# Softmax weights times context in a three-layer kernel: one fp32 product rewritten as three fp32r products on split operands, from chunk 6 on

## The chip, the cores and the metric

One NeuronCore of a Trainium2 chip runs the whole program. The metric is the device time of one execution in microseconds (us); less is better. The engines are TensorE (PE, with its weight loads as PEld), VectorE (DVE), ScalarE (ACT), GpSimd (POOL) and SyncE (SP, which here only issues DMAs). Each engine works through its own list of instructions strictly in order; they are tied together by semaphores.

## The reference

Three layers act on `x` (4 batches of 128 tokens, 512 wide). The second (16-head causal attention on compressed features) and the third (a mixture of 16 experts with shared blocks) follow on the first; the change is in the first, cross attention on a context of 2048 rows of 384 per batch:

```
query = LN(x) @ Wq + bq ; key = ctx @ Wk + bk ; value = ctx @ Wv + bv
weights = softmax(query @ key.T / sqrt(512))
x = x + weights @ value
```

The kernel multiplies the softmax weights with the raw context first (128x2048 by 2048x384 for each batch) and with `Wv` afterwards. It is this product, weights times natural context, that the change rewrites.

## The kernel before

**Numbers.** Inputs are fp32. A matmul on fp32 operands is listed as two records in the trace. Elsewhere the kernel splits both operands into a high part, rounded to fp32r, and a low part, the rest, and sums three fp32r products (`split_mm`, L1580: high x low, high x high, low x high). ACT makes the high parts by a copy, DVE (sometimes POOL) the low parts by subtraction.

**Chunks.** The context is handled in 16 chunks g of 512 rows (4 to a batch). Each chunk is loaded twice by SP: transposed (`ring_T`, 4 places, L481) for the scores, and natural (`ring`, 3 places, L474) for the product. Scores use split operands; the product uses plain fp32: the transposed softmax weights `wT` (two buffers) times `ring`, for k in 0..3 (L1898).

**Steps.** All engines run through the same loop, `for step in range(1, TAIL)`, with TAIL = 21, each with its own list for a step. In step s, PE transposes the weights of chunk s-5 into bank `B_W` (`chunk_T`, L1843), computes the scores of chunk s-1 (`chunk_scores`), and near the end of the step multiplies the product of chunk s-5 (L1898). ACT casts the high parts of chunk s (`chunk_hi`, L752), copies `B_W` to `wT` (L894), and takes the exponents of a chunk (`chunk_weights`, L826). DVE makes the low parts of chunk s (`chunk_lo`, L1283) and adds the row constant and takes the maximum of the scores (L1392).

**Batch and head work inside the steps.** Every fourth step a batch has all its chunks. Its sums are transposed and split (`sums_hi` on ACT, L835; `sums_lo` on DVE, L1333; in steps 9, 13, 17), multiplied by `Wv` (`attended`), added to `x` (`cross_added` on DVE, L1323; steps 10, 14, 18) with the moments of the middle layer norm; POOL takes the inverse root (`inverse_root`, L598), DVE applies it (`normalise`, L1079) and PE transposes the rows (`rows_T`, L1589). One step later come `compress`, `moments_2`, `inverse_root_2` (POOL, L620), `normalise_2` and `compressed_T` (PE, L1779; steps 11, 15, 19), then keys, queries and values. From step 13 on each step also has one unit u of 4 heads: `pair_scores` for two units at a time (L1738), masks and maximum on DVE, `unit_exp` on ACT (L852), `unit_weights` on POOL (L627), `unit_T` on PE (also through `B_W`), `unit_copy` on ACT. In step 17 ACT casts the output weights `wo_w` (L734) and DVE makes their low part (L1055).

**Orders that matter.** ACT's list for a step is: high part of the attended rows, `chunk_hi` 0 and 1 (and 2 before step 13), copy of wT, `sums_hi`, `chunk_hi` 2 (from step 13 on), exponents, `unit_copy`, casts, `unit_exp`, `rows_hi`. DVE's is: `chunk_lo`, `cross_added`, `sums_lo`, masks, `normalise`, the scores' maximum, `chunk_lo` 2, `moments_2`, `rows_lo`, and so on. SP's list alternates the loads of transposed chunk g and natural chunk g-6; each waits for its place to be free, and what is behind it waits too.

The staging buffer `raw` has two halves; weights go through it. Its second half holds nothing from the low part of `W_D` (step 6) to `load_expert(1)` after the loop.

Of the kernel before, what the change touches and what calls it, by code (L numbers as in the profile page):

```python
# [25 lines left out]
P = 128  # L26
F32 = mybir.dt.float32
F32R = mybir.dt.float32r
# [8 lines left out]
def layer_program(nc, x, ctx_in, ctxT_in, wqT, wkT, wv, wd, wu, woT, experts, bq, bk, bv, gate, bias_e,  # L37
# [41 lines left out]
    with ExitStack() as es:  # L79
# [9 lines left out]
        def sem(name):  # L89
            return es.enter_context(nc.semaphore(name))  # L90
# [88 lines left out]
        ring_T = at("ring_T", [P, RING_T, TC, CHUNK], ring_at + RING * KT * TD * 4)  # L179
        sc = at("sc", [P, 2, NKEY], s_at)  # L180
# [178 lines left out]
        ulo_first, dlo_first = sem("ulo_first"), sem("dlo_first")  # L359
        u_lo_pool, d3_in = sem("u_lo_pool"), sem("d3_in")  # L360
# [50 lines left out]
        POOL_LO = (2, 3, 4)  # L411

# [48 lines left out]
        def _(sp):  # L461
# [19 lines left out]
            def load_chunk_T(g):  # L481
                if g >= RING_T:
                    sp.wait_ge(cTlo_ok, low_parts(g - RING_T))
                    if pool_parts(g - RING_T):
                        sp.wait_ge(cTlo_pool, pool_parts(g - RING_T))
                sp.dma_start(ring_T[:, g % RING_T], ctxT_in[g].rearrange("p (t n) -> p t n", t=TC)).then_inc(ctxT_at[g % RING_T], 16)
# [33 lines left out]
            load_expert(0)  # L520
            load_expert(1)
# [49 lines left out]
        def _(pool):  # L571
# [42 lines left out]
            for g in POOL_LO:  # L614
                pool.wait_ge(cThi_ok, TC * (g + 1))
                nc.gpsimd.tensor_tensor(cT[:, g % 2, 1, TC - 1, :], ring_T[:, g % RING_T, TC - 1, :], f32(cT[:, g % 2, 0, TC - 1, :]),
                                        ALU.subtract).then_inc(cTlo_pool, 1)
# [23 lines left out]

            for step in range(1, TAIL):
                if (b := batch_at(step, POST + 1)) is not None:
                    inverse_root(norm_no["middle", b])
                if (b := batch_at(step, POST + 2)) is not None:
                    inverse_root_2(b)
                if (u := unit_at(step, 1)) is not None:
                    unit_weights(u)
                if (b := batch_at(step, WO_STEP)) is not None:
                    last_rows(b)  # L650
# [78 lines left out]
        def _(act_e):  # L729
# [17 lines left out]
            def chunk_hi(g, t):  # L747
                if t == 0:
                    act_e.wait_ge(ctxT_at[g % RING_T], 16 * (g // RING_T + 1))
                if g >= 2 and t == 0:  # L750
                    act_e.wait_ge(s_mm, g - 1)
                copy(cT[:, g % 2, 0, t, :], ring_T[:, g % RING_T, t, :]).then_inc(cThi_ok, 1)  # L752
# [75 lines left out]

            def attended_hi(b):
                act_e.wait_ge(a_mm, b + 1)  # L830
                copy(aT(b, 0), bank[B_A][:]).then_inc(ahi_ok, 1)
# [48 lines left out]
            for step in range(1, TAIL):  # L880
# [9 lines left out]
                if 0 <= g < G:  # L890
                    act_e.wait_ge(wT_mm, g + 1)
                    if g >= 2:
                        act_e.wait_ge(o_mm, g - 1)
                    copy(wT[:, g % 2, :], bank[B_W][:]).then_inc(wT_ok, 1)  # L894
# [148 lines left out]
        def _(dve):  # L1043
# [237 lines left out]
            def chunk_lo(g, t):  # L1281
                dve.wait_ge(cThi_ok, TC * g + t + 1)
                V_.tensor_tensor(cT[:, g % 2, 1, t, :], ring_T[:, g % RING_T, t, :], f32(cT[:, g % 2, 0, t, :]),  # L1283
                                 ALU.subtract).then_inc(cTlo_ok, 1)

# [291 lines left out]
        def _(pe):  # L1577
# [163 lines left out]
            def unit_T(u, step=TAIL):  # L1741
                pe.wait_ge(hw_ok, u + 1)
                if step - LAG < G:
                    pe.wait_ge(wT_ok, step - LAG + 1)
                else:
# [86 lines left out]
            def chunk_T(step):  # L1832
                g = step - LAG
                if 0 <= g < G:
                    b, c = divmod(g, NCH)
                    pe.wait_ge(w_ok, g + 1)
                    if (u := unit_at(step, 3)) is not None:
                        pe.wait_ge(hwT_ok, u + 1)
                    elif g >= 1:
                        pe.wait_ge(wT_ok, g)  # L1840
                    for k in range(KT):
                        o = c * CHUNK + k * P
                        last = nc.tensor.transpose(bank[B_W][:, k * P:(k + 1) * P], sc[:, b % 2, o:o + P], ident[:])  # L1843
# [24 lines left out]
            for step in range(1, TAIL):  # L1868
# [22 lines left out]
                if 0 <= g < G:  # L1891
# [276 lines left out]
```

## Time and profile before

| | us |
|---|---|
| three runs | 354.63, 355.23, 355.56 |
| median | 355.23 |
| profiled execution, its own time | 355.39 |
| its span, first to last instruction | 353.7 |
| granted TensorE clock, mean over the span | 0.990 |

Durations in the rows below come from the one profiled execution, whose time is the 355.39 us. Starts are counted from the start of its span. PE rows overlap, since matmuls are pipelined: the cost of one is the distance to the next start, not its listed duration. The chain that ended last follows the work back from the last instruction, at each step to what released it.

### The profile page before, as it was taken

What the parts mean: (1) busy time and instruction counts of PE and PEld (TensorE: products, weight loads), DVE (VectorE), ACT (ScalarE), POOL (GpSimd) and SP (SyncE); (2) the same over time, 40 slices, a digit from 0 to 9 for tenths busy, and PEclk for the clock granted to TensorE, in tenths of its full rate; (3) what the DMA queues carried; (4) which work ended last, traced back from release to release, by engine and by line L of the source; (5) the groups of instructions that cost most, each with busy time, mean ns of one, the idle gap of its engine ahead of it and who ended that gap; (6) DMA issues with size and microseconds to landing.
All of it is one profiled execution on the core that took longest, in us unless ns stands there. A gap on an engine that the chain in (4) does not pass through costs nothing.

```text
span 353.7 us, 7041 instructions
## 1 busy us (share of the span) xinstructions
PE 336.4 (95%) x2554; PEld 235.2 (67%) x2554; DVE 240.7 (68%) x475; ACT 189.4 (54%) x428; POOL 95.6 (27%) x114
## 2 busy tenths in 40 slices
PE   6999889999999999999899899999999999999996
PEld 4998656677777766767789789787544444444344
DVE  2875869665489728748975469980547777778486
ACT  2356666533577476565777454402246777777520
POOL 3600310000001311226575140004457544432000
PEclk9899999999999999999899999999999999999999
DMA  6984398985333227118023470799835633321663
GB/s 232 400 336 165 139 396 356 418 290 216 120 126 111 92 90 259 69 39 348 0 89 124 149 267 16 294 380 391 341 110 184 196 120 120 121 92 61 238 268 119
DMA packets 17185, 69.70 MB, mean 197 GB/s; under 512 B 2816, under 2 KB 3328, under 8 KB 14592
## 3 DMA queue, kind: packets, MB, share of 16 engines
q1 hardware_dynamic: 12768, 56.93, 43.0%
q0 software_dynamic: 3520, 11.54, 9.4%
q10 hardware_dynamic: 864, 0.79, 0.7%
q8 instruction: 21, 0.34, 0.4%
q14 instruction: 12, 0.10, 0.1%
HBM read 61.91 MB, written 7.34 MB: 196 GB/s over the span
## 4 chain that ended last, share of the span: by engine, by line
PE 76%; DVE 12%; ACT 6%; issue 3%; DMA 2%; POOL 0%; ACTq 0%; DVEq 0%
PE bank L2075 10%; PE bank L2043 10%; PE bank L1582 8%; PE bank L1898 8%; PE bank L1584 8%; PE bank L1583 8%; PE bank L2012 3%; PE bank L1791 2%; PE bank L2054 2%; PE bank L2086 2%; DMA raw<-in_wkT 2%; DVE cT L1283 2%; PE bank L1748 2%; PE bank L1843 2%; PE bank L1589 1%
## 5 line engine op out<-in xcount | busy, mean ns | idle before, releaser
L1898 PE MATMUL bank<-ring,wT 128*128 128x384 f32 x128 | 44.0, 487 | 0.7 <-ACT wT L894 0.7
L2075 PE MATMUL bank<-WX,hsT 128*32 128x512 f32 (+1 forms) x128 | 38.2, 598 | 0.0
L2043 PE MATMUL bank<-WX,xsT 128*32 128x256 f32 (+1 forms) x256 | 37.9, 380 | 0.0
L1283 DVE TENSOR_TENSOR cT<-ring_T,cT 128x512 fp32r<-128x512 f32 x45 | 31.0, 732 | 6.7 <-ACT cT L752 6.7
L1898 PEld LDWEIGHTS bank<-ring,wT 128*128 128x128 f32 x128 | 23.6, 190 | 14.2 <-ACT wT L894 0.9
L2043 PEld LDWEIGHTS bank<-WX,xsT 128*32 128x32 f32 x256 | 17.9, 110 | 21.0 <-issue 10.7
L1514 DVE COPY down_copy<-WX 128x1024 f32 x32 | 21.0, 695 | 15.8 <-PE bank L2075 15.8
L2075 PE MATMUL bank<-down_copy,hsT 128*32 128x512 f32 x192 | 30.7, 598 | 0.0
L752 ACT CAST cT<-ring_T 128x512 fp32r<-128x512 f32 x48 | 27.0, 619 | 6.5 <-PE bank L1584 6.3
L2043 PE MATMUL bank<-up_copy,xsT 128*32 128x256 f32 x384 | 30.4, 379 | 0.0
L688 POOL DMA_INDIRECT xs<-x_rows,from_row x20 | 20.0, 1001 | 37.1 <-DVE to_row L1237 25.2
L598 POOL TENSOR_TENSOR rstd<-var,mhalf 128x1 f32<-128x1 f32 x12 | 7.5, 626 | 72.3 <-DVE var L1069 72.3
L695 POOL DMA_INDIRECT y_rows<-ys,to_row x16 | 17.1, 1068 | 33.7 <-ACT ys L1000 33.7
L1507 DVE COPY up_copy<-WX 128x1024 f32 x32 | 21.1, 696 | 7.4 <-PE bank L2043 3.5
L1024 ACT COPY down_copy<-WX 128x1024 f32 x16 | 16.8, 1049 | 17.1 <-PE bank L2075 17.1
L1492 DVE COPY xsT<-bank 128x512 f32<-128x512 f32 x20 | 13.7, 685 | 14.8 <-PE bank L2012 14.8
L1582 PE MATMUL bank<-cT,qk_h 128*128 128x512 f32 x48 | 20.2, 420 | 2.4 <-DVE cT L1283 1.7
L1016 ACT COPY up_copy<-WX 128x1024 f32 x16 | 16.8, 1048 | 4.7 <-PE bank L2043 3.4
L1584 PE MATMUL bank<-cT,qk_l 128*128 128x512 f32 x48 | 18.8, 392 | 0.0
L1583 PE MATMUL bank<-cT,qk_h 128*128 128x512 f32 x48 | 18.8, 392 | 0.0
L2075 PEld LDWEIGHTS bank<-WX,hsT 128*32 128x32 f32 x128 | 7.4, 109 | 16.5 <-issue 16.5
L1582 PE MATMUL bank<-xT_l,u_w 128*128 128x256 f32 (+2 forms) x56 | 17.9, 320 | 0.0
(296 smaller groups left out, 892.3 us busy)
## 6 DMA issues: line engine op xcount, KB each, us to landing
WX<-in_experts SPq DMA_DIRECT2D x16, 1024.0 KB, 7.0
ring_T<-in_ctxT SPq DMA_DIRECT2D x16, 768.0 KB, 6.8
ring<-in_ctx SPq DMA_DIRECT2D x16, 768.0 KB, 5.0
WX<-y_rows SPq DMA_DIRECT2D x4, 1024.0 KB, 9.4
raw<-in_experts SPq DMA_DIRECT2D x3, 1024.0 KB, 4.8
raw<-in_wqT SPq DMA_DIRECT2D x4, 256.0 KB, 5.6
res<-in_x SPq DMA_DIRECT2D x4, 256.0 KB, 7.8
raw<-in_woT SPq DMA_DIRECT2D x1, 1024.0 KB, 4.9
```

The costliest lines, as they stand in the source:

```text
L688: nc.gpsimd.indirect_dma_start(out=xs[:, s % NXS, :], out_offset=None, in_=x_rows, in_offset=bass.IndirectOffsetOnAxis(ap=from_row[:, s:s ...
L695: nc.gpsimd.indirect_dma_start(out=y_rows, out_offset=bass.IndirectOffsetOnAxis(ap=to_row[:, s:s + 1], axis=0), in_=ys[:, s % NYS, :], in_ ...
L752: copy(cT[:, g % 2, 0, t, :], ring_T[:, g % RING_T, t, :]).then_inc(cThi_ok, 1)
L1283: V_.tensor_tensor(cT[:, g % 2, 1, t, :], ring_T[:, g % RING_T, t, :], f32(cT[:, g % 2, 0, t, :]), ALU.subtract).then_inc(cTlo_ok, 1)
L1507: V_.tensor_copy(up_copy[place(g, q)][:], WX[:, bass.ds(expert * (2 * HALF), HALF)]).then_inc(up_copied, 1)
L1514: V_.tensor_copy(down_copy[place(g, q)][:], WX[:, bass.ds(expert * (2 * HALF) + HALF, HALF)]).then_inc(down_copied, 1)
L1582: mm(dst, a[0], b[1], start=start, stop=False)
L1583: mm(dst, a[0], b[0], start=False, stop=False)
L1584: return mm(dst, a[1], b[0], start=False, stop=stop)
L1898: last = mm(bank[B_O][:, 0:TD], wT[:, g % 2, k * P:(k + 1) * P], ring[:, g % RING, k, :], start=(c == 0 and k == 0), stop=(c == NCH - 1 an ...
L2043: last = mm(bank[B_H[g % 2]][q * SLOT:(q + 1) * SLOT, 0:IC * P], xsT[:, g % 2, c * P + q * SLOT:c * P + (q + 1) * SLOT], w, start=c == 0, ...
L2075: last = mm(bank[B_Y[g % 2]][q * SLOT:(q + 1) * SLOT, :], hsT[:, g % 2, m * P + q * SLOT:m * P + (q + 1) * SLOT], w, start=m == 0, stop=m ...
```

## The change

From chunk 6 on (`SPLIT = 6`) the product of weights and context is made by `split_mm` from four operands: high and low part of wT, high and low part of the natural chunk. Chunks 0 to 5 stay as they are. The high parts of the context get two places, one in the second half of `raw` (even chunks), one in the fourth place of `ring_T` (odd chunks), so that `ring_T` has three places from chunk 8 on (`slot_T`). The low part is written over the chunk in `ring`. The two buffers of wT become its high and low part, so that the copy of wT waits for the product before.

New work for each of ten chunks: on ACT two copies of half a chunk, 128x768 (`context_hi`), a step ahead of the product, right behind wT's copy; on POOL two subtractions of 128x768 (`context_low`), the first at the head of the step's list, the second after `unit_weights`; on DVE one subtraction of 128x512 from `B_W` (`weights_lo`), after `chunk_lo` and ahead of `cross_added`; on PE 12 fp32r matmuls for 4 fp32 ones. `unit_T` and the next `chunk_T` also wait for `weights_lo`, because they write `B_W`. `load_expert(1)` waits for the product of chunk 14.

```diff
+        ring_lo = at("ring_lo", [P, RING, KT, TD], ring_at, F32R)
+        ctx_hi_even = at("ctx_hi_even", [P, KT, TD], raw_at + 2 * HALF * 4, F32R)
+        ctx_hi_odd = at("ctx_hi_odd", [P, KT, TD], ring_at + (RING + RING_T - 1) * KT * TD * 4, F32R)
+        wT_r = at("wT_r", [P, 2, CHUNK], wt_at, F32R)
...
+        SPLIT = 6
+        HALF_KT = KT // 2
+        def slot_T(g):
+            return g % RING_T if g < 2 * RING_T else (g - 2 * RING_T) % (RING_T - 1)
+        def ctx_hi(g):
+            return ctx_hi_even if g % 2 == 0 else ctx_hi_odd
...
             def load_chunk_T(g):
                 if g >= RING_T:
-                    sp.wait_ge(cTlo_ok, low_parts(g - RING_T))
-                    if pool_parts(g - RING_T):
-                        sp.wait_ge(cTlo_pool, pool_parts(g - RING_T))
-                sp.dma_start(ring_T[:, g % RING_T], ...)
+                    v = max(q for q in range(g) if slot_T(q) == slot_T(g))
+                    sp.wait_ge(cTlo_ok, low_parts(v))
+                    if pool_parts(v):
+                        sp.wait_ge(cTlo_pool, pool_parts(v))
+                sp.dma_start(ring_T[:, slot_T(g)], ...)
...
             load_expert(0)
+            sp.wait_ge(o_mm, G - 1)
             load_expert(1)
...
+            def context_low(g, h):                                    # POOL
+                pool.wait_ge(ctxhi_ok, 2 * (g - SPLIT) + h + 1)
+                k = slice(h * HALF_KT, (h + 1) * HALF_KT)
+                nc.gpsimd.tensor_tensor(ring_lo[:, g % RING, k, :], ring[:, g % RING, k, :], f32(ctx_hi(g)[:, k, :]),
+                                        ALU.subtract).then_inc(ctxlo_ok, 1)
             for step in range(1, TAIL):
+                g = step - LAG + 1
+                if SPLIT <= g < G:
+                    context_low(g, 0)
                 ... inverse_root, inverse_root_2, unit_weights ...
+                if SPLIT <= g < G:
+                    context_low(g, 1)
...
+            def context_hi(g):                                        # ACT
+                act_e.wait_ge(ctx_at[g % RING], 16 * (g // RING + 1))
+                if g >= SPLIT + 2:
+                    act_e.wait_ge(o_mm, g - 1)
+                elif g % 2 == 0:
+                    act_e.wait_ge(w_lo, LO_D)
+                else:
+                    act_e.wait_ge(cTlo_ok, low_parts(2 * RING_T - 1))
+                for h in range(2):
+                    k = slice(h * HALF_KT, (h + 1) * HALF_KT)
+                    copy(ctx_hi(g)[:, k, :], ring[:, g % RING, k, :]).then_inc(ctxhi_ok, 1)
...
                     act_e.wait_ge(wT_mm, g + 1)
-                    if g >= 2:
-                        act_e.wait_ge(o_mm, g - 1)
-                    copy(wT[:, g % 2, :], bank[B_W][:]).then_inc(wT_ok, 1)
+                    if g >= SPLIT:
+                        act_e.wait_ge(o_mm, g)
+                        copy(wT_r[:, 0, :], bank[B_W][:]).then_inc(wT_ok, 1)
+                    else:
+                        ... as before ...
+                if SPLIT <= g + 1 < G:
+                    context_hi(g + 1)
                 if (b := batch_at(step, POST)) is not None:
                     sums_hi(b)
...
+            def weights_lo(g):                                        # DVE
+                dve.wait_ge(wT_ok, g + 1)
+                V_.tensor_tensor(wT_r[:, 1, :], bank[B_W][:], f32(wT_r[:, 0, :]), ALU.subtract).then_inc(wTlo_ok, 1)
...
+                if SPLIT <= step - LAG < G:
+                    weights_lo(step - LAG)
                 if (b := batch_at(step, POST + 1)) is not None:
                     cross_added(b)
...
+                    if g >= SPLIT:                                    # PE
+                        pe.wait_ge(wTlo_ok, g - SPLIT + 1)
                     for k in range(KT):
-                        last = mm(bank[B_O][:, 0:TD], wT[:, g % 2, k * P:(k + 1) * P], ring[:, g % RING, k, :],
-                                  start=(c == 0 and k == 0), stop=(c == NCH - 1 and k == KT - 1))
+                        first, final = c == 0 and k == 0, c == NCH - 1 and k == KT - 1
+                        if g < SPLIT:
+                            ... as before ...
+                            continue
+                        pe.wait_ge(ctxlo_ok, 2 * (g - SPLIT) + k // HALF_KT + 1)
+                        o = slice(k * P, (k + 1) * P)
+                        last = split_mm(bank[B_O][:, 0:TD], (wT_r[:, 0, o], wT_r[:, 1, o]),
+                                        (ctx_hi(g)[:, k, :], ring_lo[:, g % RING, k, :]), first, final)
```

## Rows read from the trace of the kernel before

**Rows 1.** The page, busy us, share of the span, instructions.

```profile
PE 336.4 (95%) x2554; PEld 235.2 (67%) x2554; DVE 240.7 (68%) x475; ACT 189.4 (54%) x428; POOL 95.6 (27%) x114
```

**Rows 2.** The page, the chain that ended last, share by engine.

```profile
PE 76%; DVE 12%; ACT 6%; issue 3%; DMA 2%; POOL 0%; ACTq 0%; DVEq 0%
```

**Rows 3.** Windows, steps 13-14, 17-18: length; PE, PEld, DVE, ACT, POOL busy; clock; DMA.

```profile
95.20:111.00 15.80, 15.24 (x78) 10.71 (x76) 12.86 (x26) 10.51 (x33) 1.56 (x2) 1.00 0.31 101
...
127.80:142.20 14.40, 12.66 (x99) 8.81 (x98) 9.38 (x16) 10.22 (x30) 2.63 (x3) 1.00 0.67 238
```

**Rows 4.** The chain in order of time, steps 13-14: start, us, what.

```profile
96.54 0.81 ACT sc L826 x2
...
98.87 0.39 ACT DW L835
...
105.33 0.61 DVE res L1323
...
109.28 1.52 ACT hw L852 x8
...
110.93 1.16 PE bank L1738 x16
```

**Rows 5.** The chain in order of time, steps 17-18.

```profile
132.06 1.81 ACT wo_w L734
...
136.10 0.69 DVE res L1323
...
142.17 1.16 PE bank L1738 x16
```

**Rows 6.** Timeline of PE near the start: fp32r passes of 386 columns.

```profile
18.14 0.33 PE L1613 MATMUL bank<-wk,UW 128*128 128x386 f32 x1
...
19.19 0.34 PE L1613 MATMUL bank<-wk,UW 128*128 128x386 f32 x1
```

**Rows 7.** The chain in order of time, end of step 11.

```profile
85.25 2.58 PE bank L1898 x8
...
87.87 0.44 PE bank L1779 x2
```

**Rows 8.** Groups by line and shape: count, busy us, mean ns.

```profile
L752 ACT CAST cT<-ring_T 128x512 fp32r<-128x512 f32 x48 | 27.0, 619 | 6.5 <-PE bank L1584 6.3
...
L738 ACT CAST u_w<-raw 128x1024 fp32r<-128x1024 f32 x4 | 4.1, 1043 | 0.0
...
L1084 DVE TENSOR_TENSOR xT_l<-bank,xT_h 128x512 fp32r<-128x512 f32 x12 | 8.2, 687 | 11.1 <-ACT xT_h L745 11.1
...
L639 POOL TENSOR_TENSOR u_w<-raw,u_w 128x512 fp32r<-128x512 f32 x4 | 5.1, 1276 | 0.0
...
L683 POOL TENSOR_TENSOR u_w<-raw,u_w 128x1024 fp32r<-128x1024 f32 x1 | 2.4, 2403 | 0.0
```

**Rows 9.** Timeline of step 10: start, us, engine, line, operation.

```profile
76.24 0.59 ACT L894 COPY wT<-bank 128x512 f32<-128x512 f32 x1 [3.37 <-PE bank L1843]
...
77.70 0.55 POOL L598 TENSOR_TENSOR rstd<-var,mhalf 128x1 f32<-128x1 f32 x1 [32.00 <-DVE var L1069]
...
78.36 0.55 DVE L1079 TENSOR_SCALAR xn<-res,mv,rstd 128x512 f32<-128x512 f32 x1 [0.74 <-POOL rstd L598]
...
80.70 0.60 PE L1589 MATMUL bank<-ident,xn 128*128 128x128 f32 x4
```

**Rows 10.** Timeline after the loop, POOL and DVE side by side.

```profile
165.53 1.26 POOL L639 TENSOR_TENSOR u_w<-raw,u_w 128x512 fp32r<-128x512 f32 x1
...
165.69 1.38 DVE L1079 TENSOR_SCALAR xn<-res,mv,rstd 128x512 f32<-128x512 f32 x1 [0.17 <-POOL rstd L598]
```

**Rows 11.** A load's issue (timeline); loads by KB and us to landing.

```profile
70.25 0.33 SPq L486 DMA_DIRECT2D ring_T<-in_ctxT  x1
...
ring_T<-in_ctxT SPq DMA_DIRECT2D x16, 768.0 KB, 6.8
ring<-in_ctx SPq DMA_DIRECT2D x16, 768.0 KB, 5.0
```

More of the change, by code:

```diff
@@ L359, in layer_program @@
         ulo_first, dlo_first = sem("ulo_first"), sem("dlo_first")
+        ctxhi_ok, ctxlo_ok, wTlo_ok = sem("ctxhi_ok"), sem("ctxlo_ok"), sem("wTlo_ok")
         u_lo_pool, d3_in = sem("u_lo_pool"), sem("d3_in")
@@ L482, in load_chunk_T @@
                 if g >= RING_T:
-                    sp.wait_ge(cTlo_ok, low_parts(g - RING_T))
-                    if pool_parts(g - RING_T):
-                        sp.wait_ge(cTlo_pool, pool_parts(g - RING_T))
-                sp.dma_start(ring_T[:, g % RING_T], ctxT_in[g].rearrange("p (t n) -> p t n", t=TC)).then_inc(ctxT_at[g % RING_T], 16)
+                    v = max(q for q in range(g) if slot_T(q) == slot_T(g))
+                    sp.wait_ge(cTlo_ok, low_parts(v))
+                    if pool_parts(v):
+                        sp.wait_ge(cTlo_pool, pool_parts(v))
+                sp.dma_start(ring_T[:, slot_T(g)], ctxT_in[g].rearrange("p (t n) -> p t n", t=TC)).then_inc(ctxT_at[slot_T(g)], 16)
             def load_item(n, src, cols):
@@ L615, in _ @@
                 pool.wait_ge(cThi_ok, TC * (g + 1))
-                nc.gpsimd.tensor_tensor(cT[:, g % 2, 1, TC - 1, :], ring_T[:, g % RING_T, TC - 1, :], f32(cT[:, g % 2, 0, TC - 1, :]),
+                nc.gpsimd.tensor_tensor(cT[:, g % 2, 1, TC - 1, :], ring_T[:, slot_T(g), TC - 1, :], f32(cT[:, g % 2, 0, TC - 1, :]),
                                         ALU.subtract).then_inc(cTlo_pool, 1)
@@ L748, in chunk_hi @@
                 if t == 0:
-                    act_e.wait_ge(ctxT_at[g % RING_T], 16 * (g // RING_T + 1))
+                    act_e.wait_ge(ctxT_at[slot_T(g)], 16 * (1 + sum(slot_T(q) == slot_T(g) for q in range(g))))
                 if g >= 2 and t == 0:
                     act_e.wait_ge(s_mm, g - 1)
-                copy(cT[:, g % 2, 0, t, :], ring_T[:, g % RING_T, t, :]).then_inc(cThi_ok, 1)
+                copy(cT[:, g % 2, 0, t, :], ring_T[:, slot_T(g), t, :]).then_inc(cThi_ok, 1)
             def squares(e):
@@ L891, in _ @@
                     act_e.wait_ge(wT_mm, g + 1)
-                    if g >= 2:
-                        act_e.wait_ge(o_mm, g - 1)
-                    copy(wT[:, g % 2, :], bank[B_W][:]).then_inc(wT_ok, 1)
+                    if g >= SPLIT:
+                        act_e.wait_ge(o_mm, g)
+                        copy(wT_r[:, 0, :], bank[B_W][:]).then_inc(wT_ok, 1)
+                    else:
+                        if g >= 2:
+                            act_e.wait_ge(o_mm, g - 1)
+                        copy(wT[:, g % 2, :], bank[B_W][:]).then_inc(wT_ok, 1)
+                if SPLIT <= g + 1 < G:
+                    context_hi(g + 1)
                 if (b := batch_at(step, POST)) is not None:
@@ L1282, in chunk_lo @@
                 dve.wait_ge(cThi_ok, TC * g + t + 1)
-                V_.tensor_tensor(cT[:, g % 2, 1, t, :], ring_T[:, g % RING_T, t, :], f32(cT[:, g % 2, 0, t, :]),
+                V_.tensor_tensor(cT[:, g % 2, 1, t, :], ring_T[:, slot_T(g), t, :], f32(cT[:, g % 2, 0, t, :]),
                                  ALU.subtract).then_inc(cTlo_ok, 1)
+            def weights_lo(g):
+                dve.wait_ge(wT_ok, g + 1)
+                V_.tensor_tensor(wT_r[:, 1, :], bank[B_W][:], f32(wT_r[:, 0, :]), ALU.subtract).then_inc(wTlo_ok, 1)
             for t in range(TC):
@@ L1744, in unit_T @@
                     pe.wait_ge(wT_ok, step - LAG + 1)
+                    if step - LAG >= SPLIT:
+                        pe.wait_ge(wTlo_ok, step - LAG - SPLIT + 1)
                 else:
@@ L1840, in chunk_T @@
                         pe.wait_ge(wT_ok, g)
+                        if g > SPLIT:
+                            pe.wait_ge(wTlo_ok, g - SPLIT)
                     for k in range(KT):
@@ L1896, in _ @@
                         pe.wait_ge(o_ok, b)
+                    if g >= SPLIT:
+                        pe.wait_ge(wTlo_ok, g - SPLIT + 1)
                     for k in range(KT):
-                        last = mm(bank[B_O][:, 0:TD], wT[:, g % 2, k * P:(k + 1) * P], ring[:, g % RING, k, :],
-                                  start=(c == 0 and k == 0), stop=(c == NCH - 1 and k == KT - 1))
+                        first, final = c == 0 and k == 0, c == NCH - 1 and k == KT - 1
+                        if g < SPLIT:
+                            last = mm(bank[B_O][:, 0:TD], wT[:, g % 2, k * P:(k + 1) * P], ring[:, g % RING, k, :],
+                                      start=first, stop=final)
+                            continue
[3 more added lines that the diff above has]
+                                        (ctx_hi(g)[:, k, :], ring_lo[:, g % RING, k, :]), first, final)
                     last.then_inc(o_mm, 1)
```

## The prediction

> **What bounds the kernel now.** I read the page first: PE is busy 95% of the span [rows 1] and carries 76% of the chain that ended last [rows 2]. That invites the thought that every microsecond taken off PE is won. The stretch that the change touches says otherwise. Its steps 10 to 20 run from about 75 to 158 us. I call "step s" one turn of the loop over `TAIL`: PE transposes and multiplies chunk s-5, takes scores of chunk s-1, and does batch or head work between. The windows, which I read next, show that in steps 13-14 DVE is busy 12.86 and ACT 10.51 of 15.8 us, and in steps 17-18 PE has 1.7 us idle [rows 3]. The chain, read in order of time, shows why. In steps 13-14 it leaves PE: it goes from the exponent on ACT at 96.54 through the copies of `sums_hi` (98.87), then DVE to `cross_added` (105.33) and back to ACT for `unit_exp(1)` (109.28), and enters PE only at `pair_scores(2)`, 110.93 [rows 4]. Steps 17-18 are the same: ACT's `wo_w` cast, DVE's `cross_added`, `pair_scores(6)` at 142.17 [rows 5]. PE is kept busy beside this, but it can't run ahead. So work added to ACT and DVE there counts in full, and work taken from PE there counts nothing.
>
> **PE's gain.** A chunk's product is now 8 passes in 2.58 us [rows 7]. It becomes 12 fp32r passes of 384 columns. No such pass is in the trace with 384 columns, but seven passes of 386 columns in a row start from 18.14 to 19.19 (first and last shown): 1.05 / 6 = 0.175 us each [rows 6]. 12 x 0.175 = 2.10, so 0.48 us less a chunk and 4.8 us for ten chunks, if PE were always the limit. I credit it only in steps 12, 16, 19 and 20, where what follows the product is PE's own: 4 x 0.48 = 1.9 us. In the other steps with a split product PE then waits for a result that doesn't come sooner.
>
> **What ACT gets.** `context_hi` adds two copies of 128x768 a chunk, right behind the copy of wT and ahead of `sums_hi` and the exponent. The trace has 128x512 at 0.62 and 128x1024 at 1.04 us [rows 8]; halfway is 0.83, 1.66 for both (bounds 1.24 and 2.09).
>
> **What DVE gets.** `weights_lo`, from PSUM, as the 128x512 subtraction of 0.69 us [rows 8]. It stands after `chunk_lo` and ahead of `cross_added`, `sums_lo`, the masks and `moments_2`, all of which queue behind it; and it waits for wT, so for PE's transposes and for whatever ACT does first.
>
> **What POOL gets.** Two `context_low` of 128x768 a chunk. 128x512 takes 1.28 and 128x1024 2.40 us [rows 8]; halfway 1.84 (these are the bounds). POOL was nearly idle here, but the first half stands ahead of `inverse_root`, `inverse_root_2` and `unit_weights`, and waits for ACT.
>
> **POOL against DVE.** There is one row that shows such neighbours: at 165.53 POOL begins a 1.26 us subtraction right behind an `inverse_root`, and the `normalise` that this root released takes 1.38 us instead of its 0.55 [rows 9, 10]; it ends 0.28 us after POOL's instruction. The change sets up just this sequence in steps 10 and 14, root and then second half of `context_low`. I take it that `normalise` waits there. The Trainium skill, "SBUF — State Buffer", Who interferes with whom, states the rule: a DVE operation that takes the port pair shared with GpSimd, or has two SBUF inputs, waits for the whole GpSimd instruction that started first. The row above agrees. With the rule the sum below has 2.9 us for it; if the two engines were independent it would have none.
>
> **The sum, step by step.** *Step 10* (+1.75). wT's copy ends at 76.83, the first half of `context_hi(6)` at about 77.7. POOL takes `context_low` first, so the root that ran at 77.70 runs from 79.6 to 80.2. That alone is almost covered, since `normalise` ended at 78.91 and PE asks for it only at 80.70 [rows 9]: 0.3 us past. But the second half then holds POOL from 80.25 to 82.1, `normalise` ends at 82.4 and `rows_T` starts at 82.45: 1.45 us more.
> *Step 11* (+0.7). Now PE comes out of the product 0.04 us before the normalised rows let `compressed_T` start (85.25 + 2.58 against 87.87) [rows 7]. `weights_lo` delays `moments_2` and all behind it by 0.7. PE's earlier end becomes idle time.
> *Steps 13-14* (+3.05). `sums_hi` is 1.66 later; DVE's `sums_lo`, the mask of unit 0, `unit_exp(0)` and ACT's next casts follow. wT of chunk 9 comes behind those, `weights_lo(9)` (0.69) behind wT, `cross_added` behind that, two handoffs more: about 0.25, by the 0.11 from POOL's root (77.70 + 0.55) to `normalise` (78.36) [rows 9]. 1.66 + 0.69 + 0.25 = 2.6 on a chain without slack [rows 4]. `normalise` held by `context_low(10)` adds about 0.45; the rest of that wait is under `unit_exp(1)`.
> *Step 15* (+1.4). `compressed_T` again waits for DVE: 0.8 for `weights_lo` and its handoff, 0.6 because the late rows of step 14 also delay DVE.
> *Steps 17-18* (+3.0). As 13-14: 1.66 ahead of `sums_hi` and so of the 1.81 us cast of `wo_w`, then `weights_lo(13)` ahead of `cross_added`, 0.25 of handoffs: 2.6 [rows 5]. The subtraction of `wo_w` (two SBUF inputs) meets a `context_low`: 0.4.
> 1.75 + 0.7 + 3.05 + 1.4 + 3.0 - 1.9 = +8.0 us, of it 2.9 from POOL holding DVE and 5.1 without.
>
> **At nothing.** wT's copy now waits for the product before, which PE has done before it transposes the next chunk. `load_expert(1)` waits for the second to last product, but ACT casts that block only after the last one; a late start is several microseconds of cover. The transposed ring has three places from chunk 8 on, so its loads come a step later, still two steps ahead of use. What gets nearer is the natural ring, queued behind them on SP: chunk 6 is issued behind the load that now waits for the low parts of chunk 9, so at about 70.6 (the load at 70.25 waits for the same parts today and shows when they are done) [rows 11]. Its load takes 5.0 us at the median beside the 6.8 of its neighbour [rows 11], so it lands at 75.6 to 77.4 and ACT asks at 76.83: nothing to 0.6 us, and I take 0.
>
> The profiled execution took 355.39 us for a span of 353.7; the median of the runs is 355.23. 355.4 + 8.0 = 363.4 on the first, 363.2 beside the median.
>
> **The rivals.** *PE is the bound after all* (faster, 14%). One mechanism: ACT's two copies are absorbed in its idle time and DVE's mask chain doesn't move. For it: PE's 95%; ACT is idle for a third of steps 13-14 (10.51 of 15.8 us busy [rows 3]). Against: the chain there runs over ACT's and DVE's work in its order, and `sums_hi` feeds it [rows 4]. It decides if the chain of steps 13-14 has 2.6 us of slack that the view does not show. Then 355.2 - 4.8 = 350.4, or 353 with half of it.
> *No port wait* (16%). All delays as above but DVE passes POOL: +5.1, 360.3; the point is whether `normalise` starts before the second half of `context_low`.
> *The loads decide* (8%). Chunks 6, 8 and 9 land a microsecond or two after ACT asks; ACT blocks with the exponent behind it: +10 to +12, 366. Against: by the medians it is 0.6 us at most.
> *The split saves nothing*: were a pass as dear as one of 512 columns, 12 would be no faster than 8. The row of 386 columns is against it; it would move my sum by 1.9 only.
> A balance of delay and gain within 0.3% (about what a measurement of this kernel can tell from no change, 1.1 us) has 5%. My forecast itself has 57%.
>
> **How the numbers follow.** Faster is the first rival alone, 0.14; same 0.05; slower 0.81. My forecast's own range: low prices on ACT (1.24) take 0.8 off, on POOL 0.3, and no port wait 2.9: 359.2. High prices add 0.8 for ACT and 2.2 for POOL (two halves in step 10, one each in 14 and 18): 366.3. For 8 in 10 the range goes down into the first rival, 353.0, and up to 367.0 for the loads.
>
> **What would show it.** On PE: L1898 gone for ten chunks, three fp32r forms at 0.175 a pass, and more idle time in 75-158 in spite of less work, ahead of `rows_T` of the middle norm, `compressed_T`, and the pair scores of units 2 and 6. On DVE: a `normalise` of over 1 us beside POOL; 0.7 for `weights_lo`, and `cross_added` two to three microseconds after `attended` ends. On ACT: 0.8 for each copy with no wait for a DMA ahead of it; from the last product to the end the same time as before. I am wrong if the chain through steps 13-14 and 17-18 still runs over PE, or if PE's idle time there doesn't grow.

## The result, and the profile after

Slower: 364.67 us at the median of four runs (364.10 to 368.21) beside 355.29 before, ratio 1.029, 95% interval 1.0263 to 1.0317. The prediction was 363.2, 353.0 to 367.0, slower with 0.81. The profiled execution took 365.08 us for a span of 363.3, mean clock 0.981 (0.990 before).

The page after: engines, the chain by engine, then the groups of the new work and `normalise` (L1125, L1079 before).

```profile
PE 335.9 (92%) x2594; PEld 244.3 (67%) x2594; DVE 249.9 (69%) x485; ACT 203.7 (56%) x448; POOL 131.6 (36%) x134
...
PE 70%; DVE 15%; ACT 6%; DMA 3%; issue 3%; POOL 1%; ACTq 0%; SPq 0%; DVEq 0%
...
L662 POOL TENSOR_TENSOR ring_lo<-ring,ctx_hi_even 128x768 fp32r<-128x768 f32 x10 | 18.2, 1826 | 44.0 <-ACT ctx_hi_even L867 44.0
...
L867 ACT CAST ctx_hi_even<-ring 128x768 fp32r<-128x768 f32 x10 | 7.9, 843 | 0.6 <-DMA ring<-in_ctx 0.6
...
L1334 DVE TENSOR_TENSOR wT_r<-bank,wT_r 128x512 fp32r<-128x512 f32 x10 | 6.9, 689 | 7.6 <-ACT wT_r L934 7.6
L1125 DVE TENSOR_SCALAR xn<-res,mv,rstd 128x512 f32<-128x512 f32 x12 | 9.8, 816 | 6.3 <-POOL rstd L615 6.3
```

PE's busy time hardly moved against [rows 1]; DVE has 9.2, ACT 14.3 and POOL 36.0 us more, and on the chain PE has six points less of the span, DVE three more, DMA and POOL one more each [rows 2]. The prices are those of the prediction: 0.84 for a half of `context_hi` (0.83), 1.83 for `context_low` (1.84), 0.69 for `weights_lo`.

Windows after: steps 13-14, then 15, then 17-18 (columns as in [rows 3]).

```profile
97.20:116.00 18.80, 15.18 (x86) 12.05 (x85) 15.00 (x28) 13.12 (x36) 9.62 (x7) 0.97 0.46 173
116.00:126.90 10.90, 10.40 (x58) 9.09 (x58) 7.71 (x19) 6.90 (x18) 3.36 (x3) 0.74 0.01 4
135.10:152.70 17.60, 13.17 (x104) 11.45 (x105) 11.12 (x18) 12.96 (x34) 8.48 (x7) 0.90 0.43 150
```

Steps 13-14 hold the same PE work (15.18 against 15.24 us) in 18.8 us instead of 15.8 [rows 3]. The granted clock, the number behind POOL's, is 0.74 in step 15 and 0.90 in 17-18; before it was 1.00 in 13-14 and 17-18. Step by step, by the first start of the same PE work in both traces (`chunk_T` opens step 10 at 75.60 before and at 75.44 after, so PE enters the table 0.16 us early):

| up to the start of | before | after | shift | this stretch | predicted |
|---|---|---|---|---|---|
| `rows_T`, step 10 | 80.70 | 82.63 | +1.93 | +1.93 | +1.75 |
| `compressed_T`, step 11 | 87.87 | 90.23 | +2.36 | +0.43 | +0.7 |
| `values`, step 12 | 95.00 | 97.03 | +2.03 | -0.33 | -0.48 |
| `pair_scores(2)`, steps 13-14 | 110.93 | 115.93 | +5.00 | +2.97 | +3.05 |
| `compressed_T`, step 15 | 119.23 | 126.90 | +7.67 | +2.67 | +1.4 |
| `values`, step 16 | 126.81 | 134.02 | +7.21 | -0.46 | -0.48 |
| `pair_scores(6)`, steps 17-18 | 142.17 | 152.73 | +10.56 | +3.35 | +3.0 |
| `sums_T(3)`, steps 19-20 | 158.94 | 169.01 | +10.07 | -0.49 | -0.96 |

Step 10 after, DVE, ACT and POOL by start (compare [rows 9]):

```profile
77.29 1.57 ACT L867 CAST ctx_hi_even<-ring 128x768 fp32r<-128x768 f32 x2 [0.62 <-DMA ring<-in_ctx]
...
78.20 1.81 POOL L662 TENSOR_TENSOR ring_lo<-ring,ctx_hi_even 128x768 fp32r<-128x768 f32 x1 [32.66 <-ACT ctx_hi_even L867]
79.97 0.55 POOL L615 TENSOR_TENSOR rstd<-var,mhalf 128x1 f32<-128x1 f32 x1
80.49 1.80 POOL L662 TENSOR_TENSOR ring_lo<-ring,ctx_hi_even 128x768 fp32r<-128x768 f32 x1
80.63 1.94 DVE L1125 TENSOR_SCALAR xn<-res,mv,rstd 128x512 f32<-128x512 f32 x1 [3.16 <-POOL rstd L615]
```

The root, forecast for 79.6, runs at 79.97; `normalise` takes 1.94 instead of 0.55 us and ends at 82.57, 0.28 after POOL's instruction, as in [rows 10]. ACT's copy at the head of this sequence waited 0.62 us for the load of chunk 6, and the work on POOL and DVE behind it came that much later.

The chain through step 14 after (start, us, what):

```profile
100.89 1.46 ACT ctx_hi_odd L867 x2
102.36 0.39 ACT DW L875
...
108.74 0.68 DVE wT_r L1334
109.42 0.61 DVE res L1373
...
113.25 1.59 DVE xn L1125
114.84 0.04 issue
114.88 1.12 PE bank L1641 x4
116.00 1.15 PE bank L1790 x7
```

It is [rows 4] with the three new pieces in it: `context_hi` ahead of `sums_hi`, `weights_lo` ahead of `cross_added`, and a held `normalise`. PE's transposes and `pair_scores` after it are long in their own right: 1.12 us at 114.88 for what took 0.60 in step 10 before [rows 9]. That is the half clock: it was granted 0.50 from 114.9 to 116.0.

DVE in steps 17-18 after:

```profile
142.57 2.73 DVE L1101 TENSOR_TENSOR wo_w<-raw,wo_w 128x2048 fp32r<-128x2048 f32 x1 [0.25 <-ACT wo_w L762]
146.05 0.69 DVE L1334 TENSOR_TENSOR wT_r<-bank,wT_r 128x512 fp32r<-128x512 f32 x1 [0.75 <-ACT wT_r L934]
146.66 0.68 DVE L1373 TENSOR_TENSOR res<-bank,res 128x512 f32<-128x512 f32 x1
```

`wo_w` is 2.73 long (2.29 before, beside an idle POOL), and `weights_lo` waits 0.75 for wT. That wT comes by way of PE, as the chain through these steps shows:

```profile
137.74 0.70 DVE wT_r L1334
...
138.58 0.94 PE bank L1802 x4
139.51 0.32 PE bank L1634
...
144.96 0.45 PE bank L1899 x4
145.43 0.59 ACT wT_r L934
...
146.66 0.69 DVE res L1373
```

`unit_T` (L1802) waits 1.17 us for `weights_lo(12)`. The product behind it begins at half clock, 0.32 us a pass, and `chunk_T` (L1899), the copy of wT, `weights_lo(13)` and `cross_added` (L1373) follow. Before, the chain went over ACT's cast and DVE here [rows 5].

### The profile page after: what moved, and what is told of

It is laid out like the page before. It is cut to its first block, busy times and chain, and to the rows that moved or that the text cites. A ratio compares the mean times of both kernels' runs of the same rounds, so it can differ in the third digit from the quotient of the medians.

```text
span 363.3 us, 7191 instructions
## 1 busy us (share of the span) xinstructions
PE 335.9 (92%) x2594; PEld 244.3 (67%) x2594; DVE 249.9 (69%) x485; ACT 203.7 (56%) x448; POOL 131.6 (36%) x134
## 4 chain that ended last, share of the span: by engine, by line
PE 70%; DVE 15%; ACT 6%; DMA 3%; issue 3%; POOL 1%; ACTq 0%; SPq 0%; DVEq 0%
PE bank L2140 10%; PE bank L2108 10%; PE bank L1634 8%; PE bank L1636 8%; PE bank L1635 8%; PE bank L1958 3%; PE bank L2077 2%; DVE cT L1329 2%; PE bank L1845 2%; PE bank L2119 2%; PE bank L2151 2%; DMA ring<-in_ctx 2%; PE bank L1802 2%; DMA raw<-in_wkT 2%; DVE xn L1125 2%
## 5 line engine op out<-in xcount | busy, mean ns | idle before, releaser
L662 POOL TENSOR_TENSOR ring_lo<-ring,ctx_hi_even 128x768 fp32r<-128x768 f32 x10 | 18.2, 1826 | 44.0 <-ACT ctx_hi_even L867 44.0
L662 POOL TENSOR_TENSOR ring_lo<-ring,ctx_hi_odd 128x768 fp32r<-128x768 f32 x10 | 18.3, 1838 | 20.5 <-ACT ctx_hi_odd L867 20.5
L1634 PE MATMUL bank<-cT,qk_h 128*128 128x512 f32 x48 | 20.8, 434 | 2.4 <-DVE cT L1329 1.7
L1635 PE MATMUL bank<-cT,qk_h 128*128 128x512 f32 x48 | 19.3, 402 | 0.0
L1636 PE MATMUL bank<-xT_h,u_w 128*128 128x256 f32 (+2 forms) x56 | 17.5, 312 | 0.0
```

The costliest lines, as they stand in the source:

```text
L662: nc.gpsimd.tensor_tensor(ring_lo[:, g % RING, k, :], ring[:, g % RING, k, :], f32(ctx_hi(g)[:, k, :]), ALU.subtract).then_inc(ctxlo_ok, 1)
L1634: mm(dst, a[0], b[1], start=start, stop=False)
L1635: mm(dst, a[0], b[0], start=False, stop=False)
L1636: return mm(dst, a[1], b[0], start=False, stop=stop)
```

## The experiments

The theory: work added to the ordered chain of ACT and DVE, and POOL holding DVE, are the loss; PE's gain is real but nearly worthless there; and, new from the trace, PE's clock halves behind some of its waits. The rivals: the loads and orders, or the 12 passes themselves; the amount of the work and not its place.

**Orders alone, and PE's part alone.**

```diff
-        SPLIT = 6                      # e5
+        SPLIT = G
```
```diff
 # e9: no context_hi, context_low, weights_lo; two buffers of wT
-    split_mm(..., (wT_r[:, 0, o], wT_r[:, 1, o]), (ctx_hi(g)[:, k, :], ring_lo[:, g % RING, k, :]), ...)
+    split_mm(..., (wT_r[:, g % 2, o], wT_r[:, g % 2, o]), (wv_w[:, 0, k*TD:(k+1)*TD], wv_w[:, 1, k*TD:(k+1)*TD]), ...)
```

> SPLIT = G, so that no chunk is split: plain fp32 product with two buffers of wT as before, no added work on any engine. What stays of the change is the transposed ring with three places from chunk 8 on and load_expert(1) waiting for the product of chunk 14. The prediction put these at nothing: within 0.3% of before. The rival (loads that come later cost the time) gives up to the whole 9 us.

Measured 354.99 us, ratio 1.0005 (0.9987 to 1.0023): the smaller ring and the later `load_expert(1)` cost nothing that these runs can tell. The edit has no `context_hi`, so it doesn't show what it costs to ask for the natural chunk a step earlier.

> Only PE's part of the change: 12 fp32r passes of 384 columns for each chunk from 6 on, with nothing added on ACT, DVE and POOL and two buffers of wT as before. The operands are the fp32r copy of wT twice and the high and low part of Wv in the place of the context chunk, so that the product of these chunks is left out and only its passes stand. The prediction credits the passes in four steps alone, 1.9 us: ratio 0.9947. The first rival (PE is the bound in all ten steps) gives 4.8 us: ratio 0.9865. If the passes save nothing: 1.000.

Measured 354.98 us, ratio 1.0003 (0.9980 to 1.0025). So even with nothing added the split pays nothing that can be measured, and the rival of 4.8 us is out by far. Its trace, of an execution of 353.53 us, shows where the gain goes. PE's waits in 100:160, first of before, then of this run (`pair_scores` is L1738 there and L1781 here, `sums_T` L1756 and L1799; total, times, longest):

```profile
PE bank L1748 <- ACT wT L894: 1.2, 2, 0.8
PE bank L1738 <- ACT hw L852: 0.5, 2, 0.3
...
PE bank L1756 <- DVE onorm L1418: 0.3, 1, 0.3
```
```profile
PE bank L1781 <- ACT hw L887: 1.7, 2, 1.2
PE bank L1791 <- ACT wT_r L929: 1.2, 2, 0.8
PE bank L1799 <- DVE onorm L1461: 0.8, 1, 0.8
```

Each product is 0.46 us shorter there. In 13-14 and 17-18 the two gains of each become a longer wait of `pair_scores` (1.7 against 0.5 us), the one in step 20 a wait for `onorm`. By the shift of PE's starts 1.4 us, those of steps 12, 16 and 19, are kept; the ten runs, 353.24 to 357.47 us, don't show them as a shorter time, so at this size the trace of one execution is not the time of the kernel.

**One cost taken away at a time.**

```diff
-                if SPLIT <= g < G:                        # e1: POOL, both places
-                    context_low(g, h)
```
```diff
-    copy(ctx_hi(g)[:, k, :], ring[:, g % RING, k, :])     # e10: ACT
+    copy(ctx_hi(g)[:, h * HALF_KT, 0:8], ring[:, g % RING, h * HALF_KT, 0:8])
```
```diff
-                if SPLIT <= step - LAG < G:               # e11: DVE
-                    weights_lo(step - LAG)
```

> This kernel is the changed one without POOL's context_low; the product takes the high part of the context in the place of the low part, so the correction by the low part is left out. ACT's copies, weights_lo, the 12 fp32r passes and the waits on them stay. The theory of the prediction (POOL's subtractions delay the root and hold DVE's normalise) gives 364.7 - 2.9 = 361.8 us, with normalise back at 0.55 us in steps 10 and 14 and rows_T of step 10 about 1.8 earlier. If the half clock behind step 14 comes from PE's idle time there, it goes too, another 2.6: 359.2. The rival (POOL's work runs beside DVE and costs nothing, ACT and weights_lo are the whole loss) gives 364.2 to 365.

> The changed kernel with ACT's context_hi cut to 8 columns a half, so that its place and its waits stay and about 1.3 us a chunk go. POOL's context_low has the same size and place (ring minus ring), and its result stands for both parts in the product, so the context is left out of the product of these chunks. By the prediction the copies carry 1.66 us on each of the two ordered stretches (13-14 and 17-18): 364.7 - 3.3 = 361.4, ratio 1.019; with the half clock behind them gone 2 to 4 us more, ratio 1.008 to 1.013. The rival (ACT's copies are absorbed in its idle time): ratio 1.027 to 1.030.

> The changed kernel without DVE's weights_lo and without the waits on it; the high part of wT stands for the low part, so its correction is left out. By the prediction it carries 0.7 in step 11, 0.69 and about 0.25 of handoffs in 13-14 and in 17-18, 0.8 in step 15: 3.4 us, so 361.3, ratio 1.0195; with the half clock gone, less. The rival (only ACT and POOL count, DVE has room): ratio 1.026 to 1.030.

| without | us | ratio (95%) | less than 1.029, in us |
|---|---|---|---|
| `context_low` (e1) | 360.13 | 1.0156 (1.0132 to 1.0180) | 4.8 |
| `context_hi` (e10) | 360.13 | 1.0131 (1.0088 to 1.0174) | 5.6 |
| `weights_lo` (e11) | 363.76 | 1.0257 (1.0242 to 1.0272) | 1.2 |

The last column is the difference of the ratios times the time of before on that chip (the change itself was timed on another). It sums to 11.6, more than the whole loss (10.3 by the ratio, 9.4 by the medians): the costs overlap. Without `context_low`, `rows_T` of step 10 starts 5.10 us after `chunk_T`, as before, with a `normalise` of 0.55; without `context_hi` it does so too: `normalise` is still held there (1.61 us), but from 78.99 to 80.60, just ahead of PE's 80.65. In e10 POOL's subtraction, of one chunk from itself, took 1.47 and not 1.83 us, so that run lightened POOL too, and its 5.6 is an upper bound for ACT. Its four runs also spread from 357.85 to 362.31 us, and the trace is of the last. Even so the two runs reject "POOL runs beside DVE" and "ACT's copies are absorbed". `weights_lo` was worth a third of the expected 3.4: 1.0195 lies outside the interval, the rival's 1.026 reaches into it. In e11's trace step 11 still loses 0.44 (`context_low` ahead of the root does it alone, as `weights_lo` alone does in e1, 0.34), and what 17-18 win goes again in a new stretch of half clock, 147 to 152, granted 0.73.

What three stretches lost against before, by the same starts as in the table of the result (each column is one execution; e3 follows below):

| stretch | the change | no `context_low` (e1) | no `context_hi` (e10) | no `weights_lo` (e11) | waits of PE filled (e3) |
|---|---|---|---|---|---|
| steps 13-14 | +2.97 | +2.05 | +1.55 | +2.42 | +2.56 |
| step 15 | +2.67 | +1.61 | +2.83 | +1.58 | +0.85 |
| steps 17-18 | +3.35 | +3.36 | +3.33 | +1.92 | +2.51 |

In steps 13-14 each cost gives back its part, 0.92, 1.42 and 0.55, together 2.89 of the 2.97. In steps 17-18 `context_low` and `context_hi` give back nothing, and `weights_lo` 1.43. In e1 and e10 the chain runs there as in the change: `unit_T` waits 1.17 and 1.16 us for `weights_lo(12)`, the product behind it runs at half clock (granted 0.54 and 0.55 over 3.7 us), and `weights_lo(13)` then waits 1.19 and 1.96 us for wT. Without `weights_lo` the way over `context_hi` and the cast of `wo_w` is left.

**PE kept busy, and PE slower.**

```diff
+                if step == 17:                            # e3
+                    warm(16, bank[1], 4)
                 ... unit_T(u, step)
...
+                if step == 14:
+                    warm(13, bank[B_S], 10)               # 10 fp32r passes of 512 columns, read by nothing
                 ... rows_T(norm_no["middle", b], bank[B_POST])
```
```diff
 # e4: all added work and waits stay
-    split_mm(..., (wT_r[:, 0, o], wT_r[:, 1, o]), (ctx_hi(g)[:, k, :], ring_lo[:, g % RING, k, :]), ...)
+    mm(..., f32(wT_r[:, 0, o]), f32(ctx_hi(g)[:, k, :]), ...)
```

> The changed kernel with matmuls that nothing reads, in PE's idle time: 10 fp32r passes of 512 columns ahead of rows_T in step 14 (2.1 us of the 2.85 that PE waits there) and 4 ahead of unit_T in step 17 (0.85 of 1.17). If the half clock from 116 to 121.6 and from 138.6 to 142 follows from PE's idleness, both stretches run at full clock: 2.6 and up to 1.8 us less, 360.3 to 362.1, with granted clock 1.00 in the windows of steps 15 and 17. The rival (the clock falls for another cause, or the time is set by DVE's and ACT's chain there anyway) gives 364.5 to 365.5 and windows of 0.74 and 0.90 again.

Measured 361.37 us, ratio 1.0197 (1.0171 to 1.0222), which by the ratios is 3.3 us faster than the change, for more work on PE, and within what was expected. By the table above 0.41 us of it are in steps 13-14, 1.82 in step 15 and 0.84 in steps 17-18. Windows of the changed kernel, then of this run:

```profile
112.00:116.00 4.00, 1.15 (x7) 0.79 (x6) 3.97 (x6) 1.51 (x8) 2.54 (x2) 0.86 0.53 197
116.00:120.00 4.00, 4.00 (x23) 3.58 (x24) 2.28 (x5) 2.53 (x5) 0.00 (x0) 0.50 0.00 0
```
```profile
112.00:116.00 4.00, 3.49 (x31) 2.66 (x30) 3.91 (x6) 3.20 (x12) 1.23 (x1) 1.00 0.48 175
116.00:120.00 4.00, 4.00 (x27) 3.63 (x26) 3.93 (x8) 4.00 (x10) 1.84 (x1) 1.00 0.03 6
139.00:143.00 4.00, 1.75 (x13) 1.38 (x12) 3.97 (x4) 4.00 (x13) 1.92 (x2) 1.00 0.74 214
143.00:147.00 4.00, 4.00 (x25) 3.65 (x28) 3.57 (x8) 0.95 (x4) 1.24 (x3) 0.57 0.57 233
```

With PE busy 3.49 of 4 us ahead of step 15 the clock is 1.00 where it was 0.50. In steps 17-18 the half clock came back later, behind the next wait (1.75 of 4 us busy, then 0.57).

> All added work on ACT, DVE and POOL and every wait stays, but PE multiplies in plain fp32 again, 4 matmuls a chunk, from the high parts alone (the corrections by the low parts are left out). This puts a number on what the split gives PE. The prediction credited 4 x 0.48 = 1.9 us, so 366.6; if PE were the limit in all ten steps, 4.8 more, 369.5; if the 12 passes save nothing, or if what is saved is spent in waits everywhere, 364.7.

Measured 364.17 us, ratio 1.0282 (1.0227 to 1.0338): giving the split up on PE while paying for it elsewhere changes nothing that this run can tell, as the theory has it for a gain of 1 or 2 us; 369.5 is rejected, 364.7 and 366.6 aren't told apart.

**Another place for the same work.**

```diff
-                if SPLIT <= g + 1 < G:                    # ACT, behind wT's copy
-                    context_hi(g + 1)
...
 # e2: at the end of the step's list; e6: just ahead of unit_exp
+                if SPLIT <= g + 1 < G:
+                    context_hi(g + 1)
 # POOL: both context_low behind the roots and unit_weights (e2: behind last_rows too; e6: behind normalise of the middle norm too)
```

> All of the change is kept, only the places in the lists move: ACT's context_hi goes to the end of its step, behind the exponents and casts, and POOL's two context_low to the end of its step, behind the roots and last_rows. weights_lo stays. If the loss is the place of this work on the ordered chain, steps 10 (1.9), 13-14 (1.66 + 0.45) and 17-18 (1.66 + 0.4) give back about 6 us and the half clock may go with PE's waits: 356 to 359 us, with rows_T of step 10 within 0.7 of before and PE not waiting at the product. The rival (the operands are then too late, PE waits at the product for context_low; or the amount of work on ACT and POOL counts, not its place) gives 363 to 368.

> All of the change is kept; ACT's context_hi moves behind the exponents, unit_copy and casts, just ahead of unit_exp (not to the very end as in the run before), and POOL's two context_low behind the roots and unit_weights, in steps 10, 14 and 18 also behind the normalise of the middle norm. weights_lo stays. If context_hi ahead of sums_hi and POOL holding normalise are the loss, steps 10 (1.9), 13-14 (1.6 to 2.6) and 17-18 (1.6) give back 5 us or more: 357 to 360, and rows_T of step 10 is back at its place. The rival, which the run before suggests: chunk_lo, the subtraction with two SBUF inputs, now meets context_low and is held for its 1.8 us in each step, so that weights_lo and the product come late: 362 to 368, with chunk_lo over 0.9 us at the mean in place of 0.69.

e2 measured 385.31 us, ratio 1.0876 (1.0845 to 1.0907): far outside either forecast. e6 measured 362.71, ratio 1.0221 (1.0203 to 1.0239), 2.4 us better than the change and where its rival had it (362 to 368, `chunk_lo` over 0.9). My expectation fell in both. POOL and DVE in e2, then the group of `chunk_lo` in e2 and in e6:

```profile
82.77 4.06 POOL L662 TENSOR_TENSOR ring_lo<-ring,ctx_hi_even 128x768 fp32r<-128x768 f32 x2 [4.48 <-ACT ctx_hi_even L866]
...
83.98 4.01 DVE L1328 TENSOR_TENSOR cT<-ring_T,cT 128x512 fp32r<-128x512 f32 x3 [1.29 <-ACT cT L779]
...
L1328 DVE TENSOR_TENSOR cT<-ring_T,cT 128x512 fp32r<-128x512 f32 x15 | 20.3, 1390 | 12.6 <-ACT cT L779 12.6
```
```profile
L1330 DVE TENSOR_TENSOR cT<-ring_T,cT 128x512 fp32r<-128x512 f32 x16 | 15.0, 970 | 4.3 <-ACT cT L781 4.3
```

`chunk_lo`, 0.69 at the mean in this stretch before and after, is held to 1.39 and 0.97: now it meets `context_low`. In e2 the copies also stood behind instructions that wait for PE's last work of the step (`rows_hi`, `compressed`, `values_copy`), and PE then waits for `weights_lo` at the product, 3.57 us in step 11. So the place mattered more than I thought: the change's own was far better than that of e2, and 2.4 us worse than that of e6. (e6's trace is of an execution of 366.58 us, 3.9 above its median; only its `chunk_lo` is read from it.)

**Only where PE sets the time.** `context_hi`, `context_low` and `weights_lo` of a few chunks are put into each engine's idle time, all other chunks keep the fp32 product.

```diff
-        SPLIT = 6
+        PARTS = {7: 'odd', 11: 'odd', 14: 'even', 15: 'odd'}       # e7; e8: and 4: 'even'; e12: 11 and 14 alone
...
```

> Only the chunks 7, 11, 14 and 15 are split, whose products stand in steps 12, 16, 19 and 20, where the prediction credited 0.48 us each; all others keep the plain fp32 product. context_hi of these four stands where ACT waits (step 11 behind wT, 15 behind unit_exp, 18 ahead of unit_exp, 19 ahead of unit_copy), context_low behind unit_weights (step 11: one half ahead of the root), weights_lo behind the masks or in the wait for the root. If the theory holds (the split pays where PE sets the time and the added work stands in idle time), 4 x 0.46 - 0.3 = 1.5 us less than before: ratio 0.995 to 0.997. The rival (the added work costs wherever it stands): 1 us or more above before.

Measured 355.53 us, ratio 1.0034 (1.0010 to 1.0058), 0.3% on the wrong side, 1.2 us, as the rival had it. By its trace steps 12, 16 and 19 gain 0.36, 0.34 and 0.46; step 11 loses 0.36 by the root behind `context_low`, and at `unit_T` in step 20 0.45 is lost.

> As the run with four chunks, and chunk 4 split as well: context_hi in step 8, where ACT waits 2.67 us for the row maximum, context_low behind it, weights_lo in step 9 behind chunk_lo, the product in step 9, where PE sets the time. By the theory another 0.46 less: 353 to 353.5 if before is 355.2, ratio 0.993 to 0.996. The rival (natural chunk 4 hasn't landed in step 8, or chunk_lo is held by context_low): 0 to 2 us slower than the run with four chunks.

Measured 356.43 us, ratio 1.0046 (1.0028 to 1.0064): the rival. ACT, then DVE:

```profile
65.79 1.56 ACT L877 CAST ctx_hi_even<-ring 128x768 fp32r<-128x768 f32 x2 [2.58 <-DMA ring<-in_ctx]
...
68.61 3.46 DVE L1345 TENSOR_TENSOR cT<-ring_T,cT 128x512 fp32r<-128x512 f32 x3 [0.32 <-ACT cT L790]
```

The natural chunk lands 2.58 us after ACT asks; so `context_low` is late and meets `chunk_lo`, three of which take 3.46 instead of 1.89 us.

> As the run with four chunks, but only the chunks 11 and 14 are split, the two whose gain of 0.46 us stood to the end of the stretch in its trace without a loss beside it (chunk 7 lost 0.36 to a root held in step 11, chunk 15 0.45 to unit_T waiting for weights_lo in step 20). If that reading is right, 0.9 us less than before: ratio 0.9965 to 0.9985. The rival (a gain of this size is spent in the next wait on DVE or ACT): ratio 0.999 to 1.003.

Measured 354.25 us, ratio 0.9999 (0.9980 to 1.0019): no difference. Its trace keeps both gains, 0.35 and 0.49 us, up to `sums_T(3)`, and its fastest run is 353.34 beside 354.16 of 23 runs of before, but the times of one kernel differ by more: 353.34 to 356.33 us, with mean clocks of 1.000 to 0.985. No version here is shown to beat the kernel before.

## Why the prediction was right, and where it was off

*Step 10, and POOL holding `normalise`*: right in mechanism, 1.93 against 1.75, and e1 takes the delay away. The size is in part luck: 0.62 us of it is the load of chunk 6, which I took at 0. In the traces of e3, e4 and e11 ACT doesn't wait for that load; `rows_T` then waits 1.21 to 1.23 us, not 1.91, and starts 6.47 us after `chunk_T`, not 7.19 (5.10 before), so the work alone cost 1.37. PE and ACT in e3:

```profile
74.79 0.60 PE L1899 MATMUL bank<-ident,sc 128*128 128x128 f32 x4
75.91 1.57 ACT L867 CAST ctx_hi_even<-ring 128x768 fp32r<-128x768 f32 x2
...
81.26 0.66 PE L1641 MATMUL bank<-ident,xn 128*128 128x128 f32 x4 [1.21 <-DVE xn L1125]
```

The Trainium skill, "SBUF — State Buffer", Who interferes with whom, says that a DVE operation with two SBUF inputs, or in a mode that takes the shared port pair, blocks against a GpSimd instruction for the whole of it, and that one with at most one SBUF input outside such a mode doesn't. The traces agree: `normalise` 1.94 against 0.55 us, `chunk_lo` 1.39 against 0.69 in e2, while `cross_added`, with one input in PSUM, took 0.68 at 109.34 in the change, all of it beside a `context_low` (109.31 to 111.16), as it did before (0.68). (`weights_lo` met a `context_low` for 0.3 us at most and shows nothing here.)

The whole of `context_low` was worth 4.8 us by e1, where I had 2.9 for holding. (The holding terms of my sum, 1.45, 0.45 and 0.4, make 2.3; 2.9 comes out only with the 0.6 of late rows in step 15. The top of my own range, 363.2 + 0.8 + 2.2, is 366.2 and not 366.3.) By the starts e1 gives back 2.09 in step 10 (the load's wait is in it), 0.92 in steps 13-14, 1.06 in step 15, where I had no term for `context_low`, and nothing in steps 17-18, where I had 0.4.

*Step 11*: 0.43 for 0.7. Either of two causes alone costs about 0.4, `weights_lo` ahead of `moments_2` or the root behind `context_low`; they don't add.

*Steps 13-14*: 2.97 for 3.05, and the chain shows each piece, but with other sizes, so the sum agrees in part by luck. `context_hi` makes `sums_hi` 1.47 later (I had 1.66), and `weights_lo` adds 0.60 (I had 0.69 and 0.25 of handoffs). By `unit_exp(1)`, which ends at 114.87, `pair_scores` would start at 115.0. It starts at 115.93, behind a `rows_T` that waits for the held `normalise` (1.59) and then runs at half clock: 0.9 where I had 0.45 and nothing for the clock.

*Step 15*: the term that failed. I had 1.4 from DVE (`weights_lo` and late rows). `compressed_T` waited only 0.5 for DVE; the stretch lost 2.67, at a clock of 0.74: PE had waited 2.85 us ahead of `rows_T` and ran at half clock from 114.9 to 121.6 (granted 0.50). e3 fills most of that wait, the half clock there is gone, and the stretch loses 0.85, with `compressed_T` waiting 1.35 for DVE. So DVE's delay was there, hidden behind PE at half clock, and the half clock cost 1.82 by this run. My sum had no term for it.

*Steps 17-18*: 3.35 for 3.0 is near by luck, and the path was wrong. I had it over `context_hi` ahead of the `wo_w` cast. On DVE that cast is indeed later by about 1.4 and its low part 0.44 longer; then come 0.75 of waiting for wT and 0.61 of `weights_lo`. But e10 takes the copies away and the stretch still loses 3.33. What set the time was `unit_T` waiting for `weights_lo(12)`, which had no term in my sum, and the product at half clock behind it (passes 0.32 us apart, 139.5 to 142). The chain is on PE from 138.58 to 145.43 there, which I had named as a sign of being wrong; the other one, that PE's idle time wouldn't grow, did not come (4.43 us in place of 1.74 [rows 3]).

*PE's gain*: each product saves 0.46 to 0.48 as forecast, and only where PE sets the time. But I credited four steps and one of them, step 20, ends in a wait for `onorm`: 1.28 us of the 1.9. e9 rejects the rival that PE is the bound, in spite of the 95% on the page.

*At nothing*: e5 bears out the ring of three places and the later `load_expert(1)`. The load of chunk 6 made ACT wait 0.62 in the one trace of the change, just past the top of my 0 to 0.6 and on the chain of step 10; in e3, e4 and e11 it made it wait nothing. The loads did not decide.

The sum: +8.0 forecast, +10.07 measured up to `sums_T(3)`, of which 0.45 is given back by 174.65 us, +9.6 in the span. (There PE runs at half clock in the profiled execution of the kernel before, granted 0.52 from 167 to 170, and not in that of the change; e5, which splits nothing, shows 0.43 too.) Of the 2.1 us that I was short, 1.27 are step 15, 0.35 steps 17-18 and 0.62 PE's credit in steps 12 and 19-20; the small misses of the other steps cancel. What stays open: how the loss divides between clock and chain exactly, since every run that removes a cost also moves the half clock.

## What to carry to other kernels

An engine that is busy 95% of a span isn't the bound of each stretch: before work is moved off it, look in the chain, stretch by stretch, for the engine whose ordered list feeds it, since a saving becomes a wait there and the added work counts in full. When PE is made to wait for others, reckon that the work behind the wait may run at half clock, as it did here in steps 15 and 17. Price every wait that a new instruction adds, also that of an instruction which only shares a buffer with it (`unit_T`). And place GpSimd's work against the DVE instructions that it held here (`chunk_lo` and `wo_w`, with two SBUF inputs, and `normalise`), not against DVE's busy share: of the five other placements tried here none beat the kernel before.

## What the runs showed of the hardware that I had not expected

PE's granted clock was 0.50 (1.2 of 2.4 GHz) from 114.9 to 121.6 us, behind a wait of 2.85 us; of the 4 us from 112 to 116 PE was busy 1.15. With 3.49 busy there it stayed at 1.00 (e3). The length of one wait doesn't tell: 1.91 us ahead of `rows_T` in step 10 left it at 1.00, while 1.17 ahead of `unit_T` in step 17 was followed by 0.54 (138.5 to 142.2). The Trainium skill, "TensorE: Matmul & The Clock Gate", Part 1, says that the gate follows how busy PE has been; the first two rows agree. But listed busy time is not all of it. In the kernel before PE was busy 3.74 us of the 4 from 162.4 to 166.4, and the clock was 0.55 from 166.4 to 167.0 and 0.52 from 167 to 170; behind the same work in the change (3.72 busy, 172.05 to 176.05) it stayed at 1.00. Why is open. Matmuls that nothing reads made the kernel 3.3 us faster.

The hold between POOL and DVE goes both ways: in e2 the five pairs of `context_low` that met a `chunk_lo` took 4.05 to 4.11 us, the three that met none 3.60.
